# Second x loaded behind the constants and half split by GpSimd, with small products moved inside the mixing stage

## The chip, the cores and the metric

One core of a Trainium2 chip runs the kernel. A time is the device time of one launch in microseconds (us), and smaller is better. The core's engines each run a program of their own and meet at semaphores: TensorE (PE; its weight loads are listed as PEld), VectorE (DVE), ScalarE (ACT) and GpSimd (POOL). SyncE (SP) issues all DMAs of this kernel from one queue; 16 DMA engines carry them out.

## The reference, cut to what matters

Four conditioned layers are added in turn to x, which is 32 x 128 x 2048 (batch element, channel, position). Layers 0, 2 and 3 mix eight 128x128 weight matrices per batch element; layer 1 is a grouped convolution with 9 taps.

```python
def mixed(x, embedding, W0, b0, W1, b1, W2, b2, weight, bias_k):   # layers 0, 2, 3
    h = gelu(embedding @ W0 + b0); h = gelu(h @ W1 + b1)
    att = softmax(h @ W2 + b2, axis=-1)                 # 32 x 8
    agg_w = einsum('bk,koi->boi', att, weight[..., 0])  # 32 x 128 x 128
    return einsum('boi,bih->boh', agg_w, x) + (att @ bias_k)[:, :, None]

def conv(x, c, weight, c_weight, bias):                 # layer 1: 4 groups, 9 taps, padding 4
    ctx = einsum('nd,od->no', c, c_weight)
    return conv1d(x, weight, groups=4) + ctx[:, :, None] + bias[None, :, None]

x = x + mixed(x, cond_128, ...)   # layer 0
x = x + conv(x, cond_128, ...)    # layer 1
x = x + mixed(x, cond_128, ...)   # layer 2
x = x + mixed(x, cond_128, ...)   # layer 3
```

## The kernel before, in words

**Algebra.** The identity of each residual is folded into the weights. With a0, a2 and a3 the mixed matrices plus identity, layer 0 is `a0 x + c0`, the convolution has one added to its centre tap, and layers 2 and 3 collapse into one matrix `m`, the product of a3 and a2, for each batch element. What is left per element is: layer 0 (4 x 12 products), the convolution (4 x 36) and the product with m (4 x 12). Biases become vectors: `c0`, `d` (context plus bias of the convolution), `c2`, and `e`, the bias of the last two layers.

**Precision.** Every operand of the large products is kept as a high and a low part. "Splitting" x means a cast into the high part (`x_hi`) and a subtraction that leaves the low part (`x_lo`). A large product is then three: high by high, low by high, high by low. Each x is split in two halves, h = 0 and 1.

**The opening stage.** (1) A small network gives the attention shares (`hidden`, `logits`). (2) `attention` on PE spreads the shares over the partitions; DVE masks them into `spread`, one piece per layer. (3) `mixtures` makes a0, a2 and a3 in 24 tiles ("mixing"), four lanes of 32 rows side by side, four products per tile. ACT or DVE copies each tile out of PSUM, by the table `BY_SCALAR`; seven banks go round, so tile t waits for the copy of tile t-7. Between the products lie the small ones of c0, c2 and the spread third attention (`biases`), and of e (`bias_e`, 2 + 8 products). (4) `quad_product` multiplies a3 by a2, four elements at a time: quads 0 to 3, then layer 0 of x(0), then quads 4 to 7. (5) From then on four lanes, two steps apart, run through the 32 elements: layer 0 of element n+1, the convolution of n, the product with m of n-1 inside it.

**a0's way through DRAM.** The mixed a0 lies the wrong way round for the grouped rows, so SP saves it (`a0_pairs`; the first pair alone, the other 15 later) and reads it back four times (`a0_rep`); GpSimd splits it (`split_a0`). m goes the same way.

**The first x's.** x(0) comes in two halves at the head of the queue, and GpSimd splits both. x(1) is loaded by `load(1)`, which SP issues behind the read-back of a0's first pair; ACT casts its halves (between the first copies of m) and DVE subtracts. Behind those subtractions DVE's program has `x1_out(0)`: it writes the low part of the output of x(0)'s layer 0. `layer0_steps(1, p)` waits for piece p of it (`x1_lo_done`), since both use the same PSUM bank. From x(2) on DVE splits each x alone.

**What sets the order.** Nothing is scheduled at run time: each engine's program is written out in order, and `in_turn` takes one product from each lane in rotation. SP's queue is served in the order written, with its waits in it.

Of the kernel before, what the change touches and what calls it, by code (L numbers as in the profile page):

```python
# [9 lines left out]
ACT = mybir.ActivationFunctionType  # L10
# [5 lines left out]
K = 8  # L16
PH = 4
G = 4
# [5 lines left out]
NL = 3  # L24
# [5 lines left out]
LANES = 4  # L30
MIXES = NL * NOG

BY_SCALAR = [t % 2 == 0 or t == 9 for t in range(MIXES)]
DIAGONAL = OG * (LANES - 1) + HO
DMA = 16
PAIR = 2
# [30 lines left out]
def cond_resid_kernel(nc, x, net, consts, mix, bias, conv, c_weight, w3, out):  # L67
    with ExitStack() as ctx:  # L68
# [198 lines left out]
        def _(sp):  # L267
# [56 lines left out]
            load_half(0, 1)  # L324
            sp.dma_start(w3_sb, w3.rearrange("p (k m) -> p k m", k=K)).then_inc(e_loaded, DMA)
            sp.dma_start(conv_f[:], conv).then_inc(conv_loaded, DMA)
            sp.wait_ge(d_ready, 1)
            sp.dma_start(d_dram, d_sb[:]).then_inc(d_saved, DMA)

# [1 line left out]
            sp.wait_ge(*mix_taken(NOG - 1))  # L331
            save(a0_all, a0_dram, 0, 1, a0_saved[0])
            replicate_a0(0, range(PH))
            load(1)
            save(a0_all, a0_dram, 1, B // PAIR, a0_saved[1])
            load(2)
            sp.wait_ge(d_saved, DMA)
# [31 lines left out]
        def _(pe):  # L369
# [14 lines left out]

            def attention():


                pe.wait_ge(consts_loaded, DMA)
                pe.wait_ge(shares_ready, 1)
                pe.matmul(att_ps.rearrange("p n b -> p (n b)"), shares[:].rearrange("q c k o -> q (c k o)"),  # L390
                          eye_sb[0:NB, 0:NB], start=True, stop=True).then_inc(att_made, 1)
                bias_d()
                pe.matmul(att_t_ps.rearrange("k n b -> k (n b)"), shares[:, 0, :, 0], eye_sb[0:NB, 0:NB], start=True,
                          stop=True).then_inc(att_t_made, 1)
# [51 lines left out]
                          start=True, stop=True)  # L446
                pe.matmul(c2_ps, bias_sb[:, 1, :], att_t[:, 1, :], start=True, stop=True).then_inc(c_made, 1)

            def bias_e(options):
                if 0 in options:  # L450
                    pe.wait_ge(e_loaded, DMA)
                    pe.wait_ge(c2_att_ready, 1)
                    for n in range(1, NL):
                        pe.matmul(e_ps, bias_sb[:, n, :], att_t[:, n, :], start=(n == 1), stop=False)
                for k in options:
                    mm = pe.matmul(e_ps, w3_sb[:, k, :], c2_att[:, k, :], start=False, stop=(k == K - 1))  # L456
                return mm

            def layer0_steps(n, p):

# [95 lines left out]
            logits()  # L556
            fill(8)
            attention()
            mixing = [mixtures(c) for c in range(LANES)]

            in_turn(mixing, 3 * G)
            biases()
            in_turn(mixing, 2 * G)
            bias_e(range(0, 4))
            in_turn(mixing)
            bias_e(range(4, K)).then_inc(e_made, 1)
            for m in range(4):
                quad_product(m)
            in_turn([layer0_steps(0, p) for p in range(PH)])
# [5 lines left out]
        def _(act):  # L575
# [12 lines left out]
            act.wait_ge(logits_less_max, 1)  # L588
            nc.scalar.activation(lexp[:], lsub[:], ACT.Exp, accum_out=lsum[:]).then_inc(exp_done, 1)

            def split_second_x_hi(h):
                act.wait_ge(x_loaded[1], DMA)

                act.wait_ge(x_hi_done, HALVES + h)
                nc.scalar.activation(x_parts(1, h)[0], x_sb[1][:, PER * h:PER * (h + 1)],  # L595
                                     ACT.Identity).then_inc(x_hi_done, 1)

            def x1_out(n, phases=range(PH)):
                for p in phases:
# [27 lines left out]
            for t in range(MIXES):  # L627
                if BY_SCALAR[t]:
                    mix_evacuate(t)
            m_evacuate(0)  # L630
            split_second_x_hi(0)
            m_evacuate(1)
            split_second_x_hi(1)
            m_evacuate(2)
            m_evacuate(3)
            act.wait_ge(bias_out, 1)
# [18 lines left out]
        @block.gpsimd  # L655
        def _(pool):
            nc.gpsimd.memset(ones_k[:], 1.0).then_inc(ones_set, 1)
            for j in range(2):
                for buf in (x1_hi[j], x1_lo[j]):
                    nc.gpsimd.memset(buf[:, :, 0:T + 2:T + 1].bitcast(F32), 0.0).then_inc(zero_cols, 1)  # L660

            def add_identity(n):

                pool.wait_ge(mix_loaded[n], DMA)
                for diagonal in mix_diagonal[n]:
                    nc.gpsimd.tensor_tensor(diagonal, diagonal, diagonal_sb.unsqueeze(1).to_broadcast([P, G, DIAGONAL]),
                                            ALU.add).then_inc(mix_eyed[n], 1)

            def split_first_x(h):
                pool.wait_ge(x_first[h], DMA)  # L670
                src, (hi, lo) = x_sb[0][:, PER * h:PER * (h + 1)], x_parts(0, h)
                nc.gpsimd.tensor_copy(hi, src).then_inc(x_hi_done, 1)
                pool.wait_ge(x_hi_done, h + 1)
                nc.gpsimd.tensor_tensor(lo, src, hi.bitcast(F32), ALU.subtract).then_inc(x_lo_done, 1)

            def split_a0(n):
                pair = n // PAIR
                src = a0_rep[:, pair % 2, :, n % PAIR, :]
                pool.wait_ge(a0_rep_loaded[pair % 2], DMA * PH * (pair // 2 + 1))
                wait(pool, l0_done, PH * (n - 1))  # L680
                nc.gpsimd.tensor_copy(a0_hi[n % 2][:], src).then_inc(a0_split, 1)  # L681
                pool.wait_ge(a0_split, 2 * n + 1)
                nc.gpsimd.tensor_tensor(a0_lo[n % 2][:], src, a0_hi[n % 2][:].bitcast(F32),
                                        ALU.subtract).then_inc(a0_split, 1)

            def split_m(n):
                pair = n // PAIR
                src = m_rep[:, pair % 2, :, n % PAIR, :]
                pool.wait_ge(m_rep_loaded[pair % 2], DMA * PH * (pair // 2 + 1))
                wait(pool, y_done, PH * (n - 1))  # L690
                nc.gpsimd.tensor_copy(m_hi[n % 2][:], src).then_inc(m_split, 1)
                pool.wait_ge(m_split, 2 * n + 1)
                nc.gpsimd.tensor_tensor(m_lo[n % 2][:], src, m_hi[n % 2][:].bitcast(F32),
                                        ALU.subtract).then_inc(m_split, 1)


            pool.wait_ge(consts_loaded, DMA)
            pool.wait_ge(shares_ready, 1)
            for n in range(1, NL):
                add_identity(n)  # L700
            for h in range(HALVES):
                split_first_x(h)
            split_a0(0)
            split_a0(1)
            pool.wait_ge(conv_loaded, DMA)
            for q in range(PH):

                centre = conv_f[:, PH + q, rows(q)]
                nc.gpsimd.tensor_tensor(centre, centre, eye32_sb, ALU.add).then_inc(pool_chain, 1)
            pool.wait_ge(pool_chain, PH)  # L710
            nc.gpsimd.tensor_copy(conv_hi[:], conv_f[:]).then_inc(conv_split, 1)
            pool.wait_ge(conv_split, 1)
            nc.gpsimd.tensor_tensor(conv_lo[:], conv_f[:], conv_hi[:].bitcast(F32), ALU.subtract).then_inc(conv_split, 1)
            for n in range(B):
                if n + 2 < B:
                    split_a0(n + 2)
                split_m(n)

        @block.vector
        def _(dve):  # L720
# [88 lines left out]
            dve.wait_ge(e_made, 1)  # L809
            nc.vector.tensor_copy(e_all[:], e_ps).then_inc(e_out, 1)  # L810

            split_x_lo(1, 0)
            split_x_lo(1, 1)
            dve.wait_ge(bias_out, 1)
            x1_out(0)
# [81 lines left out]
```

## Time and profile before

| what | us |
|---|---|
| median of 3 runs | 488.22 |
| lowest, highest | 486.46, 493.41 |
| the profiled execution's own time | 492.4 |
| its span, first to last instruction | 490.5 |
| PE busy in that span | 478.9 |
| DVE, ACT, POOL busy | 322.7, 249.3, 153.4 |

The profile shows one execution. Its time is 4.2 us over the median and lies inside the range of the three runs. A matmul of this kernel that reads full fp32 has two records in the trace for each product; one that reads split operands has one.

### The profile page before, as it was taken

The page shows a single profiled execution, that of the slowest core. Times are in us where ns is not written, and L with a number is a line of the kernel's source. Part 1 is how long each engine was busy: PE and PEld are TensorE (multiplying, and loading weights), DVE is VectorE, ACT ScalarE, POOL GpSimd, SP SyncE. Part 2 cuts the span into 40 slices and gives each one's busy share as a digit, 9 for nine tenths or more (in the row PEclk, how much of TensorE's full clock was granted, in tenths as well). Part 3 has the DMA queues.
Part 4 walks back from the last instruction along what each step waited for, and adds up shares of the span by engine and source line. Part 5 has one row for each costly group of instructions (what it writes and reads, how often), then busy time and mean ns, then how long its engine had stood idle before and what let it go on. Part 6 is the DMA issues. An engine that isn't in the chain of part 4 may idle for free.

```text
span 490.5 us, 17899 instructions
## 1 busy us (share of the span) xinstructions
PE 478.9 (98%) x8003; PEld 433.1 (88%) x8003; DVE 322.7 (66%) x408; ACT 249.3 (51%) x415; POOL 153.4 (31%) x151
## 2 busy tenths in 40 slices
PE   8989899999999999999999999999999999999995
PEld 8979788888888888888888888888999999999994
DVE  2666766767687676767787676768777676767423
ACT  3562455544454555544554555444545554445344
POOL 3577042423332241433223241433233142430010
PEclk9998999999999999999999999999999999999998
DMA  8697957565646777464757666464667657551124
GB/s 292 208 331 226 265 182 216 169 205 131 216 153 210 216 210 217 136 212 130 219 176 215 216 200 214 134 208 124 216 204 216 215 164 214 127 204 53 67 88 172
DMA packets 38956, 92.88 MB, mean 189 GB/s; under 512 B 4568, under 2 KB 25440, under 8 KB 34912
## 3 DMA queue, kind: packets, MB, share of 16 engines
q1 hardware_dynamic: 38880, 91.73, 60.3%
q8 instruction: 64, 1.05, 0.9%
q14 instruction: 12, 0.10, 0.1%
HBM read 53.95 MB, written 37.77 MB: 187 GB/s over the span
## 4 chain that ended last, share of the span: by engine, by line
PE 97%; issue 1%; DVE 1%; DMA 1%; DVEq 0%
PE cv_ps L495 59%; PE aux_ps L476 17%; PE aux_ps L518 16%; PE cv_ps L434 2%; PE cv_ps L421 1%; PE aux_ps L421 1%; PE cv_ps L518 1%; DVE m_all L731 1%; DMA m_rep<-in_net_dram 1%; PE cv_ps L400 0%; PE aux_ps L375 0%; PE cv_ps L375 0%; PE aux_ps L456 0%; DVEq L68 0%; PE aux_ps L390 0%
## 5 line engine op out<-in xcount | busy, mean ns | idle before, releaser
L495 PE MATMUL cv_ps<-x_hi,conv_hi 32*128 32x512 f32 x1536 | 325.4, 389 | 2.2 <-issue 2.2
L495 PE MATMUL cv_ps<-x_hi,conv_lo 32*128 32x512 f32 x1536 | 325.6, 391 | 0.0
L495 PE MATMUL cv_ps<-x_lo,conv_hi 32*128 32x512 f32 x1536 | 325.3, 391 | 0.0
L495 PEld LDWEIGHTS cv_ps<-x_hi,conv_hi 32*128 32x128 f32 x1536 | 233.6, 183 | 12.4 <-issue 2.6
L495 PEld LDWEIGHTS cv_ps<-x_lo,conv_hi 32*128 32x128 f32 x1536 | 234.1, 184 | 11.5
L495 PEld LDWEIGHTS cv_ps<-x_hi,conv_lo 32*128 32x128 f32 x1536 | 233.8, 183 | 7.3
L764 DVE SCALAR_TENSOR_TENSOR x_lo<-cv_ps,d_all,x_hi 128x512 fp32r<-128x512 f32 x128 | 87.3, 745 | 138.7 <-ACT x_hi L609 138.7
L619 ACT ACTIVATE y_all<-aux_ps,e_all 128x512 f32<-128x512 f32 x124 | 75.1, 688 | 136.4 <-PE aux_ps L518 136.4
L476 PE MATMUL aux_ps<-x_hi,a_hi 32*128 32x512 f32 x512 | 118.1, 396 | 1.6 <-issue 1.6
L476 PE MATMUL aux_ps<-x_hi,a_lo 32*128 32x512 f32 x512 | 117.5, 392 | 0.0
L476 PE MATMUL aux_ps<-x_lo,a_hi 32*128 32x512 f32 x512 | 117.5, 392 | 0.0
L518 PE MATMUL aux_ps<-x_hi,m_hi 32*128 32x512 f32 x496 | 114.6, 388 | 0.0
L518 PE MATMUL aux_ps<-x_hi,m_lo 32*128 32x512 f32 x496 | 114.2, 388 | 0.0
L518 PE MATMUL aux_ps<-x_lo,m_hi 32*128 32x512 f32 x496 | 113.7, 385 | 0.0
L609 ACT ACTIVATE x_hi<-cv_ps,d_all 128x512 fp32r<-128x512 f32 x128 | 77.5, 689 | 67.7 <-PE cv_ps L495 67.7
L738 DVE TENSOR_TENSOR x_lo<-x_sb,x_hi 128x1024 fp32r<-128x1024 f32 x62 | 89.4, 1443 | 7.3 <-ACT x_hi L595 5.2
L755 DVE SCALAR_TENSOR_TENSOR x_lo<-aux_ps,c_all,x_hi 128x512 fp32r<-128x512 f32 x128 | 87.3, 746 | 1.6
L681 POOL CAST a_hi<-a_rep 128x512 fp32r<-128x512 f32 x32 | 27.0, 845 | 189.6 <-DMA a_rep<-a_pairs 121.0
L601 ACT ACTIVATE x_hi<-aux_ps,c_all 128x512 fp32r<-128x512 f32 x128 | 77.7, 690 | 15.7 <-PE aux_ps L476 15.7
L476 PEld LDWEIGHTS aux_ps<-x_hi,a_hi 32*128 32x128 f32 x512 | 80.2, 185 | 4.8 <-issue 1.8
L476 PEld LDWEIGHTS aux_ps<-x_hi,a_lo 32*128 32x128 f32 x512 | 80.5, 187 | 3.6
L518 PEld LDWEIGHTS aux_ps<-x_hi,m_lo 32*128 32x128 f32 x496 | 79.5, 183 | 2.9
(103 smaller groups left out, 540.5 us busy)
## 6 DMA issues: line engine op xcount, KB each, us to landing
x_sb<-in_x_dram SPq DMA_DIRECT2D x31, 1024.0 KB, 6.5
out_dram<-y_all SPq DMA_DIRECT2D x62, 512.0 KB, 7.6
a_rep<-a_pairs SPq DMA_DIRECT2D x64, 128.0 KB, 7.3
m_rep<-m_pairs SPq DMA_DIRECT2D x64, 128.0 KB, 6.1
a_pairs<-a_all SPq DMA_DIRECT2D x1, 1920.0 KB, 12.5
m_pairs<-m_all SPq DMA_DIRECT2D x1, 1792.0 KB, 13.3
m_all<-in_mix_dram SPq DMA_DIRECT2D x2, 512.0 KB, 5.6
x_sb<-in_x_dram SPq DMA_DIRECT2D x2, 512.0 KB, 7.2
```

Of the source, the lines that this page charges most:

```text
L421: mm = pe.matmul(mix_ps[t % MIX_RING][:, P * j:P * (j + 1)], mix_f[layer][rows(c), G * h + j, :], spread[rows(c), layer].rearrange("p b o ...
L434: mm = pe.matmul(prep_ps[m % RING][:, P * k:P * (k + 1)], a23_all[0][:, n, :], a23_all[1][:, n, :], start=True, stop=True)
L476: mm = pe.matmul(aux_ps[:, p, :], w[n % 2][rows(p), g, :], a[rows(p), g % PER, :], start=(i == 0), stop=(i == steps - 1))
L495: mm = pe.matmul(cv_ps[:, g, :], w[rows(g), j, :], a[n % 2][rows(g), q, s:s + T], start=(i == 0), stop=(i == steps - 1))
L518: mm = pe.matmul(out_bank(n, p), w[n % 2][rows(p), g, :], a[n % 2][rows(p), g, :], start=(i == 0), stop=(i == steps - 1))
L601: nc.scalar.activation(x1_hi[n % 2][:, p, 1:T + 1], aux_ps[:, p, :], ACT.Identity, bias=c0_all[:, n:n + 1]).then_inc(x1_hi_done, 1)
L609: nc.scalar.activation(x2_hi[n % 2][:, g, :], cv_ps[:, g, :], ACT.Identity, bias=d_all[:, g, n:n + 1]).then_inc(x2_hi_done, 1)
L619: nc.scalar.activation(y_all[:, k % YBUFS, p % PER, :], bank[:, p, :], ACT.Identity, bias=e_all[:, n:n + 1]).then_inc(y_out, 1)
L681: nc.gpsimd.tensor_copy(a0_hi[n % 2][:], src).then_inc(a0_split, 1)
L738: nc.vector.tensor_tensor(lo, x_sb[n % 2][:, PER * h:PER * (h + 1)], hi.bitcast(F32), ALU.subtract).then_inc(x_lo_done, 1)
L755: nc.vector.scalar_tensor_tensor(x1_lo[n % 2][:, p, 1:T + 1], aux_ps[:, p, :], c0_all[:, n:n + 1], x1_hi[n % 2][:, p, 1:T + 1].bitcast(F32 ...
L764: nc.vector.scalar_tensor_tensor(x2_lo[n % 2][:, g, :], cv_ps[:, g, :], d_all[:, g, n:n + 1], x2_hi[n % 2][:, g, :].bitcast(F32), ALU.add, ...
```

## The change

Five edits, all ahead of the steady stage:

1. SP issues `load(1)` right behind the constants of the convolution; it no longer stands between a0's read-back and the second save of a0.
2. GpSimd splits half 0 of x(1), high and low, ahead of `split_a0(0)`. ACT casts half 1 alone, ahead of all copies of m, and DVE subtracts half 1 alone.
3. The product for `d` and the turned shares (`att_t`) leave `attention` and follow behind two rounds of mixing (`options`). One idle product of 256 columns (`fill(1)`) takes their place.
4. The ten products for `e`, before in a block of six and a block of four, are issued one per round in the last ten rounds of mixing.
5. ACT copies tile 17 of the mixing, which DVE copied before.

```diff
-BY_SCALAR = [t % 2 == 0 or t == 9 for t in range(MIXES)]
+BY_SCALAR = [t % 2 == 0 or t in (9, 17) for t in range(MIXES)]
...
             sp.dma_start(conv_f[:], conv).then_inc(conv_loaded, DMA)
+            load(1)
             sp.wait_ge(d_ready, 1)
...
             replicate_a0(0, range(PH))
-            load(1)
             save(a0_all, a0_dram, 1, B // PAIR, a0_saved[1])
...
+            def bias_e():
+
+                pe.wait_ge(e_loaded, DMA)
+                pe.wait_ge(c2_att_ready, 1)
+                for n in range(1, NL):
+                    pe.matmul(e_ps, bias_sb[:, n, :], att_t[:, n, :], start=(n == 1), stop=False)
+                    yield
+                for k in range(K):
                     mm = pe.matmul(e_ps, w3_sb[:, k, :], c2_att[:, k, :], start=False, stop=(k == K - 1))
-                return mm
+                    if k == K - 1:
+                        mm.then_inc(e_made, 1)
+                    yield
...
             attention()
+            fill(1)
             mixing = [mixtures(c) for c in range(LANES)]
 
-            in_turn(mixing, 3 * G)
+            in_turn(mixing, 2)
+            options()
+            in_turn(mixing, 10)
             biases()
-            in_turn(mixing, 2 * G)
-            bias_e(range(0, 4))
-            in_turn(mixing)
-            bias_e(range(4, K)).then_inc(e_made, 1)
+            in_turn(mixing, 5)
+            in_turn([*mixing, bias_e()])
...
+            split_second_x_hi()
             m_evacuate(0)
-            split_second_x_hi(0)
             m_evacuate(1)
-            split_second_x_hi(1)
             m_evacuate(2)
...
             for h in range(HALVES):
-                split_first_x(h)
+                split_x(0, h)
+
+            split_x(1, 0)
             split_a0(0)
...
-            split_x_lo(1, 0)
             split_x_lo(1, 1)
             dve.wait_ge(bias_out, 1)
             x1_out(0)
```

DVE at the end of the opening stage, before and then changed; `x2_hi1` and `x2_lo1` are the buffers that hold the split x(1), and `x1_lo0` is what layer 0 of x(1) waits for.

```order
L731 COPY m_all<-cv_ps 128x32x16 [waits mix_made] x2
L810 COPY e_all<-aux_ps 128x32 [waits e_made]
L738 TENSOR_TENSOR x2_lo1<-x_sb1,x2_hi1 128x1024 [waits x_lo_done,x_hi_done] x2
L755 SCALAR_TENSOR_TENSOR x1_lo0<-aux_ps,c0_all,x1_hi0 128x512 [waits x1_hi_done,bias_out]
L755 SCALAR_TENSOR_TENSOR x1_lo0<-aux_ps,c0_all,x1_hi0 128x512 [waits x1_hi_done] x3
```

```order
L737 COPY m_all<-cv_ps 128x32x16 [waits mix_made] x2
L816 COPY e_all<-aux_ps 128x32 [waits e_made]
L744 TENSOR_TENSOR x2_lo1<-x_sb1,x2_hi1 128x1024 [waits x_lo_done,x_hi_done]
L761 SCALAR_TENSOR_TENSOR x1_lo0<-aux_ps,c0_all,x1_hi0 128x512 [waits x1_hi_done,bias_out]
L761 SCALAR_TENSOR_TENSOR x1_lo0<-aux_ps,c0_all,x1_hi0 128x512 [waits x1_hi_done] x3
```

One of two subtractions of 128x1024 is gone from DVE ahead of the four pieces; the copies of m in front of it are one fewer in all (tile 17).

POOL in the same stage, before and then changed: the split of x(0)'s last half, then a0's.

```order
L672 CAST x_hi1<-x_sb0 128x1024 [waits x_first1]
L674 TENSOR_TENSOR x_lo1<-x_sb0,x_hi1 128x1024 [waits x_hi_done]
L681 CAST a0_hi0<-a0_rep 128x512 [waits a0_rep_loaded0]
L683 TENSOR_TENSOR a0_lo0<-a0_rep,a0_hi0 128x512 [waits a0_split]
L681 CAST a0_hi1<-a0_rep 128x512 [waits a0_rep_loaded0]
```

```order
L676 CAST x_hi1<-x_sb0 128x1024 [waits x_first1]
L678 TENSOR_TENSOR x_lo1<-x_sb0,x_hi1 128x1024 [waits x_hi_done]
L676 CAST x2_hi1<-x_sb1 128x1024 [waits x_loaded1]
L678 TENSOR_TENSOR x2_lo1<-x_sb1,x2_hi1 128x1024 [waits x_hi_done]
L685 CAST a0_hi0<-a0_rep 128x512 [waits a0_rep_loaded0]
```

Two instructions have come in front of a0's split, and the first of them waits for the load of x(1).

PE at the end of the mixing stage (`L421`, now `L423`, are mixing products; `L456`, now `L459`, are the products for e), before and then changed.

```order
L454 MATMUL aux_ps<-att_t,bias_sb 128x32
L456 MATMUL aux_ps<-c2_att,m_rep 128x32 x4
L421 MATMUL aux_ps<-spread,a0_rep 128x128 [waits mix_out_v]
L421 MATMUL cv_ps<-spread,a0_rep 128x128
L421 MATMUL aux_ps<-spread,a0_rep 128x128 x3
L421 MATMUL cv_ps<-spread,a0_rep 128x128 [waits mix_out_a]
```

```order
L459 MATMUL aux_ps<-c2_att,m_rep 128x32
L423 MATMUL aux_ps<-spread,a0_rep 128x128 [waits mix_out_v]
L423 MATMUL cv_ps<-spread,a0_rep 128x128
L423 MATMUL aux_ps<-spread,a0_rep 128x128 x2
L459 MATMUL aux_ps<-c2_att,m_rep 128x32
L423 MATMUL aux_ps<-spread,a0_rep 128x128
```

The block of four is taken apart; between two products for e there now lie up to four mixing products.

## Rows read from the trace of the kernel before

**Rows 1.** Page, part 1: busy us, share of the span, instructions.
```profile
PE 478.9 (98%) x8003; PEld 433.1 (88%) x8003; DVE 322.7 (66%) x408; ACT 249.3 (51%) x415; POOL 153.4 (31%) x151
```

**Rows 2.** The chain that ended last, in order: start, us, what.
```profile
10.09 2.18 PE cv_ps L421 x24
...
20.61 2.50 DVE m_all L731 x4
23.25 3.81 PE cv_ps L434 x32
...
33.82 1.64 issue
35.46 4.76 PE aux_ps L476 x35
...
58.35 2.17 issue
```

**Rows 3.** Timeline of ACT, then DVE: start, us, instruction, idle before, releaser.
```profile
27.27 1.06 ACT L595 ACTIVATE x_hi<-x_sb 128x1024 fp32r<-128x1024 f32 x1 [2.27 <-DMA x_sb<-in_x_dram]
30.62 2.43 ACT L601 ACTIVATE x_hi<-aux_ps,c_all 128x512 fp32r<-128x512 f32 x4
28.37 6.32 DVE L738 TENSOR_TENSOR x_lo<-x_sb,x_hi 128x1024 fp32r<-128x1024 f32 x2 [5.17 <-ACT x_hi L595]
34.62 2.71 DVE L755 SCALAR_TENSOR_TENSOR x_lo<-aux_ps,c_all,x_hi 128x512 fp32r<-128x512 f32 x4
```

**Rows 4.** Windows: stretch, length, busy of each engine, PEclk, DMA share, GB/s.
```profile
36.00:37.00 1.00, 1.00 (x7) 0.89 (x8) 1.00 (x3) 0.00 (x0) 0.00 (x0) 0.59 0.43 150
37.00:39.00 2.00, 2.00 (x21) 2.00 (x22) 1.97 (x3) 0.00 (x0) 1.54 (x2) 0.50 0.04 15
39.00:40.00 1.00, 1.00 (x19) 1.00 (x15) 1.00 (x2) 0.00 (x0) 1.00 (x1) 0.70 0.76 227
10.00:14.00 4.00, 4.00 (x61) 3.98 (x64) 2.04 (x6) 1.36 (x3) 3.85 (x5) 1.00 1.03 424
14.00:15.00 1.00, 1.00 (x26) 1.00 (x24) 0.84 (x2) 0.71 (x2) 1.00 (x2) 1.00 0.77 286
```

**Rows 5.** Timeline of SP's queue: start and length of an issue.
```profile
6.45 0.50 SPq L326 DMA_DIRECT2D conv_f<-in_conv_dram  x1
15.95 0.33 SPq L279 DMA_DIRECT2D a_pairs<-a_all  x1
17.64 1.76 SPq L286 DMA_DIRECT2D a_rep<-a_pairs  x4
19.45 0.43 SPq L275 DMA_DIRECT2D x_sb<-in_x_dram  x1
```

**Rows 6.** DMA issues: KB each, median us from issue to landing.
```profile
conv_f<-in_conv_dram SPq DMA_DIRECT2D x1, 768.0 KB, 9.2
```

**Rows 7.** Timeline of PE and DVE in the mixing stage.
```profile
9.14 0.53 PE L404 MATMUL aux_ps<-m_rep,cw_sb 128*128 128x32 f32 x2
9.39 0.69 DVE L769 TENSOR_TENSOR spread<-aux_ps,consts_sb 128x128 f32<-128x128 f32 x3 [0.90 <-PE aux_ps L390]
21.85 1.08 PE L456 MATMUL aux_ps<-c_att,m_rep 128*128 128x32 f32 x8
```

**Rows 8.** Timeline of POOL.
```profile
15.92 2.36 POOL L674 TENSOR_TENSOR x_lo<-x_sb,x_hi 128x1024 fp32r<-128x1024 f32 x1
23.04 0.61 POOL L681 CAST a_hi<-a_rep 128x512 fp32r<-128x512 f32 x1 [4.76 <-DMA a_rep<-a_pairs]
23.73 1.27 POOL L683 TENSOR_TENSOR a_lo<-a_rep,a_hi 128x512 fp32r<-128x512 f32 x1
```

**Rows 9.** One line's instructions: DVE's subtractions, durations ns min/median/max.
```profile
L738 DVE TENSOR_TENSOR x_lo<-x_sb,x_hi x62: 1224/1226/4284, 28.4 to 450.0; 128x1024 fp32r<-128x1024 f32 x62
```

**Rows 10.** Mixing products (line 421): durations ns min/median/max; one answer until 12 us, one from 16.1 us.
```profile
L421 PE MATMUL cv_ps<-spread,m_all x26: 416/416/577, 10.0 to 11.9; 32*128 32x128 f32 x26
...
L421 PE MATMUL cv_ps<-spread,m_all x22: 270/270/372, 16.2 to 18.4; 32*128 32x128 f32 x22
```

## What was predicted before the change was run

> **What bounds the kernel now.** I read the page first, then the chain of waits, then the timeline of each engine around the places where the chain leaves PE. PE is busy 98% of the span [rows 1]: the steady stage is bound by PE alone, and the change doesn't touch it. What an edit of the opening can give lies in the pieces of the chain that are not PE at full speed. The chain has three of them [rows 2]: 2.50 us of DVE's copies of the last mixing tiles, 1.64 us of standstill at 33.82, and 2.17 us at 58.35.
>
> The piece at 33.82 is the one that the change aims at. The chain calls it "issue", so its cause must be read from the order of the instructions. Layer 0 of x(1) may not begin before the first low piece of x(0)'s output. DVE begins these four pieces at 34.62 and needs 2.71 us for them, 0.68 each [rows 3], so the first is there at 35.30; PE goes on at 35.46 [rows 2]. Their input was there long before: ACT's first high piece began at 30.62. DVE was busy from 28.37 to 34.69 with the two subtractions of x(1) [rows 3], and these began late since x(1) landed late: ACT's cast sat idle for the DMA until 27.27 [rows 3]. One of the two took 4.28 us where the median is 1.23 [rows 9].
>
> The standstill has a tail. The four lanes start one by one as DVE delivers, and the granted clock then falls: 0.59 of full in the microsecond from 36, 0.50 for two more, 0.70 in the next [rows 4]. 0.50 is the lower level, 1.2 GHz instead of 2.4. In full-speed work that is 0.41 + 1.00 + 0.30 = 1.7 us lost.
>
> **The change part by part.**
>
> *x(1) loaded early.* The queue is full until about 14.8: a DMA share of 1.03 at 424 GB/s until 14, then 0.77 of one microsecond [rows 4], and the convolution's constants land at 6.45 + 9.2 = 15.65 [rows 5, 6]. x(1) is 1 MB; at 424 GB/s it adds 2.5 us, so the engines are free at 17.3 and x(1) is there at about 18.1 instead of 27.27. It was issued at 19.45 before; the second save of a0 gets that slot, and everything behind it comes up to 2.5 us sooner. The first that waits for it is layer 0 of x(2), a whole convolution later: zero.
>
> *POOL's two new instructions.* The subtraction takes 2.36 us, as on x(0); the cast I estimate at twice the 0.61 of a 128x512 one, 1.2 [rows 8]. From 18.1 the pair ends at 21.7. POOL stands idle 4.76 us before a0's split at 23.04 [rows 8], so this costs nothing as long as x(1) lands before about 19.6. a0's split of the first element ends at 23.73 + 1.27 = 25.00, and PE wants it at 23.25 + 3.81 = 27.06 [rows 2, 8]: 2 us of slack.
>
> *a0's first save.* It was issued at 15.95 and its read-back at 17.64 [rows 5], on an empty queue. Now x(1) stands before it until 17.3. I take the landing of the save as 0.9 us later (0 if it overtakes, 1.7 if it starts only then and takes its 1.7 again), so the split ends at 25.9, still inside the slack.
>
> The Trainium skill speaks against this edit: "DMA: Bandwidth & Descriptors", Queues, rings and completion order, says that on each DMA engine descriptors are consumed in ring order, so the save cannot pass x(1). By that rule the gentle end, 0, is excluded; the value above doesn't rest on it.
>
> *DVE's list.* With half 0 gone to POOL and half 1 cast by ACT right behind its last tile, DVE's one subtraction begins near 23.6 and ends between 24.8 (1.23) and 27.9 (4.28) [rows 9], in either case before 30.62. The four low pieces follow ACT's high ones from 31.2 on. With the same 0.68 each the first is there at 31.9 and the fourth at 34.0, where PE wants them from about 34.3 (33.82 and the 0.5 of the two paragraphs below). **The standstill of 1.64 us and the 1.7 us of the clock go.**
>
> Beside that subtraction POOL now splits a0, where before it split the convolution's constants. The row at 4.28 was such a case [rows 9]. The Trainium skill has a rule: "GPSIMD Engine Reference", Key points, says that GpSimd shares its SBUF interfaces with VectorE and contends with instructions of two SBUF inputs. If a0's split stretched by as much as the 4.28 row, from 1.27 to some 3 us, it would end at 27.6 instead of 25.9; the stretch itself I bound by the rows (none to 3.05 us in all) and take 0.7.
>
> *d and the turned shares.* Before, they fill PE from 9.14 until mixing begins at 10.09 [rows 2, 7]. The first `spread` is ready at 9.39 + 0.28 (the group of three takes 0.69), and mixing can begin near 9.75. The two products are then done behind it, at the same price of 0.9. So the work is the same, PE stands or idles on `fill` in 9.14 to 9.75, and what follows comes up to 0.6 us later. Between 0 and +0.6, I take +0.2, since from 16 us on the copies set the pace there (seven banks, two engines) and they absorb some.
>
> *e's products one by one, tile 17.* A block of four takes 1.08 [rows 7], 0.27 each, singly the same work. Before, the block in the middle starves the copies, and DVE then has four in a row (2.50, 0.62 each) that PE's quads wait for until 23.25 [rows 2], while the last block runs from 21.85 to 22.93 [rows 7]. Now the last mixing product comes about one e-product before the end of the same PE work, 22.93 - 0.27 = 22.66; one copy of 0.62 ends at 23.3. That is no gain. Each e-product also cuts the four lanes apart: between 0 and 0.27 each for the eight, so 0 to 2.2. I take 0.3, near the lower end, since inside the block the eight records come at 1.08 / 8 = 0.135 us each, so even there little is lost to filling and draining. Tile 17 on ACT: nothing, ACT has room. Together +0.3.
>
> **Sum**, against the profiled execution's own 492.4: -1.64 - 1.7 + 0.2 + 0.3 = -2.8, so 489.6. That execution lies 4.2 over the median of 488.22. I can't see a median execution, so I subtract the same from the median, a little less because in some executions the clock may not have fallen: 488.2 - 2.6 = **485.6**.
>
> **The rivals.**
>
> 1. *The wait goes, but the clock's part was only in this execution.* The clock fell once the lanes had crept for 3 us; a run that starts otherwise may not fall. Then only 1.64 - 0.5 = 1.1 is saved: 487.1. For it speaks that the profiled run was a slow one; against it that the creeping is set by DVE and comes in all.
> 2. *a0 late (slower).* x(1) takes a0's place in the queue, POOL starts on it late, and DVE's subtraction stretches a0's split. It decides where layer 0 of x(0) would start, 27.06 + 0.5: if a0's read-back lands past 25.4 instead of 23.04, the first split (1.88) and its stretch (0.7) end at 28.0, PE stands again and, if it stands as long as it did at 33.82, the clock falls again. At a landing of 27.5 the loss is 2.5 + 1.7 = 4.2 against a gain of 3.3 - 0.5: 488.2 + 1.4 = 489.6. For it: the round trip is the one thing the early load can hurt. Against: 4.4 us later than now would have to come from 1 MB that needs 2.5.
> 3. *Mixing stays slow longer.* A mixing product takes 416 ns until 12 us and 270 ns from 16.2 [rows 10], though the granted clock is listed as 1.00 throughout. If gaps of single e-products and at 9.5 put off that change, each microsecond of delay costs half a microsecond; 4 us and the full 2.2 for the cuts cancel the gain: 488.2 - 3.3 + 0.2 + 2.2 + 2 = 489.3. The Trainium skill, "TensorE: Matmul & The Clock Gate", What's actually happening, says the default state is throttled and activity releases it; by that rule less activity there costs, more (an earlier start) gains, about 1 us either way.
> 4. *The standstill at 58.35.* PE waits 2.17 us [rows 2] with no semaphore in its order at that place. Instructions come by DMA too. In another arrangement of the traffic it may be gone: 485.6 - 2.2 = 483.4; or fall elsewhere, with no change.
> 5. *The change doesn't do what it says*: x(1) lands late all the same. Then DVE still has one subtraction less, about 1.2 to 3 us: 486.5.
>
> **Chances.** Forecast 0.50 (own range 484.3 to 487), rival 1: 0.17, rival 2: 0.10, rival 3: 0.08, rival 4: 0.12, rival 5: 0.03. The executions of before spread over 7 us by themselves, and the median of three carries 1 or 2 of that. So the range goes from rival 4's end less one, 482.5, to rivals 2 and 3, 489.8. The 2% that a measurement of this kernel can tell from no change are 9.8 us, more than any case here moves: within 2% 0.97, faster 0.02, slower 0.01.
>
> **What would show it.** Right: no "issue" piece near 34, DVE's four low pieces starting within 1 us of ACT's first high piece, a granted clock of 1.00 from 33 to 41, x(1)'s cast by POOL at 18 to 19, a0's first cast near 24. Wrong: a0's cast past 25, PE idle before layer 0 of x(0), quads later than 24.5, or mixing products still at 416 ns past 16 us. The prediction fails if a gain here is given back later, which I think unlikely, since behind 58.35 the chain has no further piece off PE worth a row [rows 2].

## The result, and the profile after

| | median us | range | executions |
|---|---|---|---|
| before | 488.96 | 486.46 to 494.75 | 22 |
| after | 493.94 | 491.77 to 496.62 | 22 |

After over before is 1.0109 [1.0089, 1.0128]: 1.1% slower, by 5.0 us in the medians, where 485.6 was forecast. The profiled execution after took 496.62, its span 494.8. Ratios here leave out executions more than 1.5% above the fastest of their kernel, while medians contain all; part of before's executions lie that high, so for kernels close to it the two can differ by half a per cent.

Page, part 1 and the clock line of part 2, to be held against [rows 1]:

```profile
PE 486.2 (98%) x8004; PEld 460.1 (93%) x8004; DVE 318.7 (64%) x406; ACT 252.1 (51%) x415; POOL 151.7 (31%) x153
PEclk9969999999999999999999999999999999999998
```

PE is no less full than before, yet busy 7.3 us longer. The busy share says nothing here. The third digit of the clock (a slice of 12.4 us from 24.7 on) says that PE was full at a lower rate. The chain, against [rows 2]:

```profile
30.07 5.93 PE cv_ps L436 x32
35.99 3.00 PE aux_ps L481 x43
38.99 3.77 PE cv_ps L436 x32
42.76 3.11 PE aux_ps L481 x42
```

The standstill near 34 is gone, as forecast: layer 0 of x(1) (42.76) follows the second quads at once. The quads start at 30.07 instead of 23.25, though, and take 5.93 instead of 3.81. The windows before them, with the columns of [rows 4]:

```profile
20.00:24.00 4.00, 4.00 (x67) 3.47 (x62) 1.79 (x3) 2.97 (x5) 3.25 (x2) 1.00 0.64 199
24.00:28.00 4.00, 4.00 (x33) 3.06 (x26) 1.38 (x2) 0.69 (x3) 2.43 (x3) 0.53 1.08 380
28.00:32.00 4.00, 3.69 (x15) 3.29 (x16) 1.95 (x3) 1.47 (x2) 3.90 (x6) 0.50 1.01 356
32.00:36.00 4.00, 4.00 (x29) 3.88 (x28) 0.00 (x0) 1.79 (x3) 3.92 (x2) 0.69 0.55 168
```

The granted clock falls from 1.00 to 0.50 (1.2 GHz instead of 2.4) while PE is listed busy 4.00 of 4.00 us. This is not the fall of [rows 4], which came behind a wait. PE's timeline shows what it does there: single products for e (`L459`, both records) with mixing products between them.

```profile
21.76 0.41 PE L459 MATMUL aux_ps<-c_att,m_rep 128*128 128x32 f32 x2
22.10 0.37 PE L423 MATMUL aux_ps<-spread,a_rep 32*128 32x128 f32 x1
...
22.53 0.41 PE L459 MATMUL aux_ps<-c_att,m_rep 128*128 128x32 f32 x2
...
27.83 0.64 PE L459 MATMUL aux_ps<-c_att,m_rep 128*128 128x32 f32 x2
...
29.12 0.64 PE L459 MATMUL aux_ps<-c_att,m_rep 128*128 128x32 f32 x2
```

A round with one product for e in it takes 0.77 us at the full clock and 1.29 at the lower one. So two costs are to be told apart: the cuts, by which I mean the breaks in the four lanes' rounds that a product of full height makes, and the clock. Behind them stand the other four edits.

### The profile page after: what moved, and what is told of

It is laid out like the page before. It is cut to its first block, busy times and chain, and to the rows that moved or that the text cites. A ratio compares the mean times of both kernels' runs of the same rounds, so it can differ in the third digit from the quotient of the medians.

```text
span 494.8 us, 17899 instructions
## 1 busy us (share of the span) xinstructions
PE 486.2 (98%) x8004; PEld 460.1 (93%) x8004; DVE 318.7 (64%) x406; ACT 252.1 (51%) x415; POOL 151.7 (31%) x153
## 3 DMA queue, kind: packets, MB, share of 16 engines
q8 instruction: 64, 1.05, 0.9%
## 4 chain that ended last, share of the span: by engine, by line
PE 98%; DMA 1%; DVE 0%; issue 0%; DVEq 0%
PE cv_ps L500 55%; PE aux_ps L481 18%; PE aux_ps L523 16%; PE cv_ps L436 2%; PE cv_ps L423 2%; PE aux_ps L423 1%; PE aux_ps L459 1%; PE cv_ps L523 1%; DMA m_rep<-in_net_dram 1%; PE cv_ps L402 0%; PE aux_ps L375 0%; PE cv_ps L375 0%; PE aux_ps L447 0%; DVEq L68 0%; DVE m_all L737 0%
## 5 line engine op out<-in xcount | busy, mean ns | idle before, releaser
L500 PE MATMUL cv_ps<-x_hi,conv_lo 32*128 32x512 f32 x1536 | 321.1, 391 | 0.7 <-issue 0.7
L500 PE MATMUL cv_ps<-x_lo,conv_hi 32*128 32x512 f32 x1536 | 320.5, 391 | 0.0
L500 PE MATMUL cv_ps<-x_hi,conv_hi 32*128 32x512 f32 x1536 | 320.5, 390 | 0.0
L481 PE MATMUL aux_ps<-x_hi,a_hi 32*128 32x512 f32 x512 | 113.6, 391 | 0.0
L481 PE MATMUL aux_ps<-x_hi,a_lo 32*128 32x512 f32 x512 | 113.3, 388 | 0.0
L481 PE MATMUL aux_ps<-x_lo,a_hi 32*128 32x512 f32 x512 | 113.3, 388 | 0.0
L744 DVE TENSOR_TENSOR x_lo<-x_sb,x_hi 128x1024 fp32r<-128x1024 f32 x61 | 84.7, 1389 | 2.1
L481 PEld LDWEIGHTS aux_ps<-x_hi,a_lo 32*128 32x128 f32 x512 | 75.9, 184 | 1.8
L481 PEld LDWEIGHTS aux_ps<-x_hi,a_hi 32*128 32x128 f32 x512 | 75.8, 183 | 1.9
L481 PEld LDWEIGHTS aux_ps<-x_lo,a_hi 32*128 32x128 f32 x512 | 75.8, 183 | 1.9
```

What stands on the lines that cost most here:

```text
L481: mm = pe.matmul(aux_ps[:, p, :], w[n % 2][rows(p), g, :], a[rows(p), g % PER, :], start=(i == 0), stop=(i == steps - 1))
L500: mm = pe.matmul(cv_ps[:, g, :], w[rows(g), j, :], a[n % 2][rows(g), q, s:s + T], start=(i == 0), stop=(i == steps - 1))
L744: nc.vector.tensor_tensor(lo, x_sb[n % 2][:, PER * h:PER * (h + 1)], hi.bitcast(F32), ALU.subtract).then_inc(x_lo_done, 1)
```

## The experiments

Diffs are against "after" or "before" as named; all kernels compute the whole reference. "Before" ran beside each. I call its executions over 490 us the long ones; the two of them that were profiled have a wait near 34 us.

**e's products in blocks again, all else as after.**

```diff
-            in_turn(mixing, 5)
-            in_turn([*mixing, bias_e()])
+            in_turn(mixing, 8)
+            for_e = bias_e()
+            in_turn([for_e], 6)
+            in_turn(mixing)
+            in_turn([for_e])
```

> The changed kernel with e's ten products in two blocks again (6 and 4, as before), all else as changed. Theory S (the single products for e are the loss: each cuts the four lanes apart, the granted clock falls to 0.5 in that stretch and stays there through the first quads): the stretch from the first product for e to the first quad goes back from 9.4 us to about 5, quads 0 to 3 from 5.9 to 3.8 us, so 6 us less than the changed kernel: about 488. Rival O (moving d and the turned shares behind two rounds puts off the rise of the clock, from about 16 us to 21 us, and that is the loss): mixing products still last 416 ns until 20 us, and the time stays within 1 us of the changed kernel's 494.

Measured 488.61 (486.56 to 491.95), 5.3 under after; ratio to before 1.000 [0.9971, 1.0029]. In its chain and windows:

```profile
23.59 3.81 PE cv_ps L436 x32
...
20.00:24.00 4.00, 3.80 (x62) 3.56 (x61) 2.06 (x4) 2.96 (x6) 3.22 (x2) 1.00 0.40 117
24.00:28.00 4.00, 4.00 (x41) 3.88 (x43) 1.22 (x1) 2.44 (x5) 2.65 (x4) 1.00 1.07 376
```

The clock stays at 1.00 and the quads take 3.81. This one edit holds the whole loss of the change; what the others cost and bring adds up to about nothing.

**`d` and the turned shares ahead of mixing again; then that and the blocks together.** In the first the diff against after is

```diff
-            fill(1)
+            options()
...
-            in_turn(mixing, 2)
-            options()
-            in_turn(mixing, 10)
+            in_turn(mixing, 12)
```

and the second has the diff above as well: the early x(1), its split by GpSimd and tile 17 are all that it keeps.

> The changed kernel with the product for d and the turned shares ahead of mixing again and without the extra idle product; e's products stay single. Theory O: the clock rises near 16 us again, mixing ends 2 to 5 us sooner, and the time goes to 488 to 490. Theory S: the clock still falls at the single products, the first quad starts at 26 us or later, and the time stays above 492.

> The changed kernel with both edits of the order on TensorE undone; the early load of x(1), its split by GpSimd, and tile 17 on ScalarE stay. If the saving that was predicted for the early x(1) is real, the wait before layer 0 of x(1) (1.64 us) and the fall of the clock behind it (1.7 us) are gone and the time is 485.5 to 486.5, below the kernel before by 3. If an early x(1) costs a0's round trip through DRAM more than it brings, the first layer 0 waits for a0's split and the time is 489 or more.

Measured 492.17 (490.76 to 493.97), 1.0076 [1.0051, 1.0102], for the first; 486.75 (485.95 to 490.07), 0.998 [0.9958, 1.0002], for the second. Single products cost 5.4 in this pair, and moving `d` and the shares costs 1.8 (after less the first) or 1.9 (the blocks less the second). The second kernel's chain has neither wait nor slow stretch:

```profile
20.72 1.90 DVE m_all L738 x3
22.62 0.14 issue
22.75 3.81 PE cv_ps L436 x32
26.56 3.38 PE aux_ps L481 x48
29.94 3.77 PE cv_ps L436 x32
33.71 3.10 PE aux_ps L481 x42
```

**Each of the two edits alone, on before.** `bias_e` and the rounds as in the change, nothing else of it; then `fill(1)` and `options()` as in the change, nothing else.

> The kernel before with e's products single as the only edit. Theory S: 3 to 6 us slower than before, 492 to 495, with a granted clock under 0.8 between 20 and 30 us. Theory O: the clock has risen by 16 us as before, the single products cost at most their own switching, and the time is within 1 us of before's 489.

> The kernel before with the product for d and the turned shares behind two rounds of mixing and one idle product in their place, nothing else. Forecast price: +0.2 us. From the profiles of e_blocks and both_back, where the first copy starts 1.14 us later (13.27 against 12.13 in before): +1 to +2 us.

The first: 492.43 (489.17 to 495.17), 1.0098 [1.0066, 1.013], 4.0 over before beside it (488.47). The second: 489.26 (487.22 to 494.92), 1.0031 [1.0002, 1.0061], 1.3 over (487.98). So the loss needs no early x(1): the granted clock falls on the kernel before too, in the windows below. The price is under 5.4, and a reason for it stands in the trace: the kernel before's own wait near 34 is gone, since PE comes to layer 0 of x(1) only at 37.87. The windows of the first:

```profile
24.00:28.00 4.00, 3.69 (x17) 3.59 (x18) 0.45 (x2) 1.42 (x2) 3.85 (x8) 0.50 1.07 381
28.00:32.00 4.00, 4.00 (x34) 3.77 (x36) 3.74 (x2) 2.86 (x5) 3.92 (x2) 0.71 1.01 378
```

For the second, the place is ACT's first copy, in before and then in the second kernel:

```profile
12.13 0.60 ACT L583 ACTIVATE a_all<-cv_ps 128x512 f32<-128x512 f32 x1 [4.14 <-PE cv_ps L421]
```

```profile
13.17 0.60 ACT L588 ACTIVATE a_all<-cv_ps 128x512 f32<-128x512 f32 x1 [5.20 <-PE cv_ps L423]
```

The products moved behind two rounds end there in the same price, but what the copies wait for comes 1.04 us later. The same stands in after (13.27); with the products back ahead it is 12.17 (e single) and 12.10 (blocks).

**How many cuts does it take?** e two products at a time, in five cuts, `d` and the shares ahead of mixing:

```diff
+            in_turn(mixing, 8)
+            for_e = bias_e()
+            in_turn([for_e], 2)
+            for _ in range(4):
+                in_turn(mixing, 2)
+                in_turn([for_e], 2)
+            in_turn(mixing)
```

> As att_first, with e's products two at a time between two rounds of mixing: five cuts instead of ten. In the profiles a round with a single product takes 0.77 us at the full clock, against about 0.25 for a round and 0.25 for a product in a block, so a cut costs 0.27. Theory C: five cuts fewer save 1.3 us, and if the clock then holds, 3 us more: 488 to 491. If only the position in the program matters and not the number of cuts: 492, as att_first.

Measured 487.99 (486.40 to 490.38), 1.0001 [0.9966, 1.0037]: 4.2 less than ten singles, 1.2 more than blocks of six and four (before itself read 487.90 beside this run and 488.47 beside those two). In its profile the clock falls in one window alone, and rises again under the quads; that execution took 490.35, at the upper end of the twelve, so a median one may lose less:

```profile
24.00:28.00 4.00, 4.00 (x24) 4.00 (x23) 1.04 (x1) 1.19 (x2) 2.24 (x3) 0.57 1.03 353
28.00:32.00 4.00, 4.00 (x59) 3.23 (x57) 0.00 (x0) 1.20 (x2) 3.78 (x8) 1.00 1.07 373
```

**Can idle work hold the clock?** e singly, and behind each of its products one 128x256 idle product into a free bank:

```diff
-            in_turn([*mixing, bias_e()])
+            def idle_beside():
+                for i in range(K + NL - 1):
...
+                    pe.matmul(mix_ps[bank % MIX_RING][:, 0:2 * P], idle_sb[:, 0:P], idle_sb[:], start=True, stop=True)
+                    yield
+            in_turn([*mixing, bias_e(), idle_beside()])
```

> As att_first (e's products single, d and turned shares ahead of mixing), with one idle product of 128x256 zeros behind each product for e: more work on TensorE, at the same number of cuts. Theory C (half of the loss is the clock, which falls because the array does so little between the cuts): the granted clock stays 1.00 from 20 to 32 us, the quads take 3.8 us instead of 6.1, and the time falls by 1.5 to 3 us from att_first's 492.2 although ten products are added. Rival P (the clock falls whatever is put there, or the loss is all the switching): the same fall of the clock and 1 to 2 us more than att_first.

Measured 494.95 (492.86 to 497.05), 1.013 [1.0077, 1.0183], 2.8 over the same kernel without them. The fall comes later (0.91 in the first window, 0.65 without the idle products) and is as deep, so the added work is paid and buys nothing:

```profile
20.00:24.00 4.00, 4.00 (x42) 3.00 (x42) 0.69 (x1) 1.79 (x3) 2.73 (x2) 0.91 0.41 108
24.00:28.00 4.00, 4.00 (x18) 3.02 (x15) 1.17 (x2) 1.54 (x2) 2.63 (x4) 0.50 1.06 369
28.00:32.00 4.00, 4.00 (x19) 3.80 (x19) 2.16 (x3) 0.60 (x1) 3.94 (x6) 0.50 1.07 383
```

**No cut at all.** All ten products behind the last mixing product, with the early x(1) (run twice), and on before alone:

```diff
-            in_turn(mixing, 5)
-            in_turn([*mixing, bias_e()])
+            in_turn(mixing)
+            in_turn([bias_e()])
```

> As both_back, with all ten products for e in one block behind the last mixing product: no cut inside mixing, and the copies of the last tiles run beside the block. Theory C: the first quad starts 0 to 0.7 us sooner than in both_back (22.75), clock 1.00, time 486 to 487. If the block of products without mixing beside it lets the clock fall (it has 32 columns each): the quads at half rate, 488 to 490.

> e_last once more (early x(1), split by GpSimd, tile 17 on ScalarE, e's products in one block at the end): 486 to 487, with a narrower spread than before, since no execution has the wait at 34 us.

> The kernel before with all ten products for e in one block behind the last mixing product, nothing else changed. If the order of e's products is worth something by itself (no starving of the copies between two blocks), 0.3 to 0.8 us under before. Its difference from e_last_b is the worth of the early x(1): 3.3 by the forecast, 1 to 1.7 if the wait at 34 us is there in some executions only.

With the early x(1): 486.52 (485.69 to 487.50), 0.997 [0.994, 0.9999], and again 486.41 (485.91 to 487.36), 0.9966 [0.9938, 0.9993]. This is the lowest median of the study: 0.3% under before, with intervals that end just below 1, and 1.5% under after. The block stands where PE would wait for the last copies anyway: the quads follow it without a wait. Its chain, from the first run, and then the block in PE's timeline:

```profile
20.48 1.90 PE aux_ps L459 x16
22.38 3.65 PE cv_ps L436 x32
```

```profile
20.41 1.97 PE L459 MATMUL aux_ps<-c_att,m_rep 128*128 128x32 f32 x16
```

On before alone: 490.93, in two groups, four executions at 485.03 to 485.40 and eight at 490.37 to 495.25; 0.9996 [0.9949, 1.0042]. Its profile fell in the upper group and has the wait at 32.48 for 2.56 us. Held against the two runs above, it gives the worth of the early load with GpSimd's split and tile 17: without them about 485.3 or 490 and more, with them 485.7 to 487.5 in all 23 executions.

**Tile 17 back on DVE, in the fastest kernel.** One entry of `BY_SCALAR` less.

> e_last with tile 17 of the mixing copied by VectorE again. If the edit was free, as priced: within 0.3 us of e_last_b. If ScalarE relieves the last copies: 0.3 to 0.7 us slower.

486.91 (486.14 to 487.74), 0.9977 [0.9958, 0.9997]: 0.4 to 0.5 more than with it on ACT, little more than the two runs of one kernel can tell.

**x(1) late, still split by GpSimd.** `load(1)` back behind a0's read-back, in the kernel with both other edits undone.

> As both_back, with the load of x(1) back at its old place behind a0's read-back; GpSimd still splits half 0, so it now waits for x(1) ahead of a0's split. If the place of the load is what saves the time: x(1) lands at 27, GpSimd's a0 split comes only behind it at 31 or later, TensorE stands before the first layer 0, and the time is 490 to 494. If the early load does nothing: 486.8.

Measured 495.37 (493.74 to 498.17), 1.0144 [1.009, 1.0198], 8.6 over its counterpart. POOL's cast of x(1) waits for the load, a0's split waits behind it, and PE stands:

```profile
26.31 1.04 POOL L677 CAST x_hi<-x_sb 128x1024 fp32r<-128x1024 f32 x1 [7.58 <-DMA x_sb<-in_x_dram]
27.43 2.34 POOL L679 TENSOR_TENSOR x_lo<-x_sb,x_hi 128x1024 fp32r<-128x1024 f32 x1
29.72 0.60 POOL L686 CAST a_hi<-a_rep 128x512 fp32r<-128x512 f32 x1
```

```profile
26.96 5.66 issue
```

Half of x(1) on POOL is only good together with the early load.

**The given kernels once more, unchanged,** to see how far one profile speaks for all executions: before twice, after once.

> The kernel before, unchanged, once more under the profiler. The first profile lay 4.2 us over the median. If the fall of the clock behind the wait at 34 us and the standstill of 2.17 us at 58 us belong to that execution and not to the kernel, one or both are missing here and the span is 485 to 488; if they belong to the kernel, both are here and the early x(1) should have brought 3.3 us, not the 1.7 that both_back measured.

> The same as before_a, a second look. The wait before layer 0 of x(1) (1.6 us) should be here in each, since it comes from the order of the loads.

> The changed kernel, unchanged, once more under the profiler. If the single products for e set the fall of the clock, it falls here too between 20 and 26 us. The first rise, at 21 us in the first profile and near 16 us in all kernels run since, is expected near 16 us here; if it is at 21 us again, moving d and the turned shares puts it off.

Before took 493.25 and 486.24. The wait near 34 is in the first, 2.62 us long, and not in the second. What differs is when x(1) lands, told by ACT's first cast of it; in order, the first and the second:

```profile
28.51 1.06 ACT L595 ACTIVATE x_hi<-x_sb 128x1024 fp32r<-128x1024 f32 x1 [3.73 <-DMA x_sb<-in_x_dram]
```

```profile
26.60 1.06 ACT L595 ACTIVATE x_hi<-x_sb 128x1024 fp32r<-128x1024 f32 x1 [1.88 <-DMA x_sb<-in_x_dram]
```

The landing alone would not reach PE. Without a stretch, by my estimate from the rows, DVE's second subtraction in the first of the two would end at 29.95 + 1.05 + 1.23 = 32.2, ACT's first high piece is there at 31.86 + 0.61 = 32.5, and a low piece takes 0.68: 33.2, before PE stops at 33.59. What holds DVE is POOL's subtraction of the convolution's constants. DVE, then POOL, in the first:

```profile
29.60 5.84 DVE L738 TENSOR_TENSOR x_lo<-x_sb,x_hi 128x1024 fp32r<-128x1024 f32 x2 [6.63 <-ACT x_hi L595]
30.06 4.30 POOL L713 TENSOR_TENSOR conv_lo<-conv_f,conv_hi 128x1536 fp32r<-128x1536 f32 x1
```

and in the second, where DVE's second subtraction has begun before POOL's:

```profile
29.12 2.20 DVE L738 TENSOR_TENSOR x_lo<-x_sb,x_hi 128x1024 fp32r<-128x1024 f32 x1 [0.20 <-ACT x_hi L595]
30.33 4.34 POOL L713 TENSOR_TENSOR conv_lo<-conv_f,conv_hi 128x1536 fp32r<-128x1536 f32 x1
```

In the five traces in which POOL's began first (the two long ones of before, `d` and the shares moved on before, e last on before, e single on before), DVE's second subtraction ended 1.08 or 1.09 us behind POOL's, at 34.28 to 35.44; here it ended at 31.32. So the landing decides which engine comes first, and that decides over a wait. This is read from six traces; no run moved POOL's subtraction alone. Of the 7.0 us between the two executions 2.6 are the wait, 3.4 the clock (0.96, 0.50 and 0.68 in the windows of 4 us from 32 to 44) and 0.55 a standstill at 60.26.

After took 493.7, with its quads at 27.73 for 6.14 us and the same fall:

```profile
20.00:24.00 4.00, 4.00 (x46) 3.21 (x46) 0.69 (x1) 2.08 (x4) 3.05 (x2) 0.80 0.48 141
24.00:28.00 4.00, 3.69 (x19) 2.81 (x14) 1.80 (x4) 1.54 (x2) 3.12 (x4) 0.50 1.08 386
28.00:32.00 4.00, 4.00 (x20) 4.00 (x20) 1.67 (x1) 1.08 (x2) 3.86 (x7) 0.50 1.00 357
32.00:36.00 4.00, 4.00 (x53) 3.56 (x55) 0.00 (x0) 1.31 (x3) 3.44 (x1) 0.92 0.86 221
```

## Why the prediction was wrong

**The sum by edits**, in medians: early x(1) with its split and tile 17 gave 486.75 - 488.47 = -1.7 (before's median over the 35 executions that ran beside them), the options cost +1.9, e's single products +5.4. That makes +5.6; measured were +5.0 against before's 488.96, and +5.5 against these 488.47. The forecast had -3.3, +0.2 and +0.3 in the same places, with tile 17 at nothing.

**The step that failed is e's products one by one**: "between 0 and 0.27 each for the eight, so 0 to 2.2. I take 0.3, near the lower end". It failed twice.

- *Its size.* A round of mixing without a product for e takes about 0.25 us (seven rounds between 20.15 and 21.85 before), a product for e 0.25 (eight in 1.97 behind the mixing). Together 0.50, where the single round takes 0.77: 0.27 a cut, the upper bound, and 2.2 for eight. In the chains less of it arrives. From the first mixing product that reads `a_rep` to the first quad pass 9.79 us with `d` and the shares ahead and e single, 5.57 with the blocks; 2.8 of the difference are the clock, so 1.5 are the cuts. The second profile of after against its kernel in blocks gives 1.5 too, e single on before 1.7. The reason for the low end was the rate of the records inside a block of like products; that says nothing of a change from full-height products to four lanes of 32 rows and back.
- *Its kind.* No term had the clock fall under a busy PE. In the second profile of after the windows lose 0.20, 0.50, 0.50 and 0.08 of 4 us each: 0.8 + 2.0 + 2.0 + 0.3 = 5.1 us of full-speed work.

For the kernel with `d` and the shares ahead these two are read against its counterpart in blocks: 1.5 for the cuts and 1.4 + 2.0 + 1.7 = 5.1 for the clock (0.65, 0.50 and 0.57 in the windows from 20 to 32), less the 0.4 by which its layer 0 of x(0) is shorter (2.99 against 3.38). That is 6.2; the two profiled executions lie 6.3 apart (492.25 and 485.95), the medians 5.4. So about a quarter of the loss is the cuts and the rest the clock.

That the single products bring the fall is shown, on both kernels; that fewer cuts bring a shorter one, too. What in the alternation the chip answers to is not: PE was listed busy all along, and idle products between did not help. The listed busy time may hide that fewer rows of the array work; that stays open.

**x(1) early.** The effect came as forecast: no wait near 34, clock 1.00 from 36 on, DVE's low pieces (39.87) 0.8 behind ACT's high ones (39.07); POOL's cast of x(1) came at 19.84, a little behind the 18 to 19 of the forecast. The cause was seen in part. The prediction laid DVE's lateness to the landing and took the row of 4.28 us as a bound; that row, DVE held by POOL's subtraction, is what made PE wait, and the early x(1) takes DVE out of POOL's way. The size was off, because the wait of [rows 2] isn't there in every execution, and the fall of the clock not behind every wait. "The creeping is set by DVE and comes in all" was wrong: in the kernel before with `d` and the shares moved, PE waits 1.66 us at 34.10 and creeps in the same way, but the clock stays, and the execution took 489.1:

```profile
36.00:40.00 4.00, 4.00 (x55) 3.41 (x58) 3.96 (x6) 0.80 (x3) 1.57 (x1) 1.00 0.37 112
```

That is rival 1's mechanism, in some executions. In the median the edit gives 1.7; against a long execution it gives 4 and more, against a short one it costs about 1 (486.4 against 485.3 with e last), and nothing here shows why.

**a0's save** lies inside its bounds: 3.1 us from issue to landing instead of 1.7, 1.4 later where 0.9 was taken. Its own issue came 1.1 later too, so a0's first cast stands at 25.44, past the 25 that the prediction had named as a sign of being wrong. SP's issues of the save and of the read-back, and then POOL:

```profile
17.09 0.33 SPq L279 DMA_DIRECT2D a_pairs<-a_all  x1
20.22 1.76 SPq L286 DMA_DIRECT2D a_rep<-a_pairs  x4
```

```profile
19.84 1.04 POOL L676 CAST x_hi<-x_sb 128x1024 fp32r<-128x1024 f32 x1 [1.38 <-DMA x_sb<-in_x_dram]
25.44 0.61 POOL L685 CAST a_hi<-a_rep 128x512 fp32r<-128x512 f32 x1 [2.12 <-DMA a_rep<-a_pairs]
```

The Trainium skill's rule of ring order ("DMA: Bandwidth & Descriptors", Queues, rings and completion order) agrees with this: the save of 128 KB did not land before x(1), whose landing released POOL at 19.84. a0's split held up nobody, since the quads came 6.8 us late. It was near to deciding, though: in one run with e in one block, layer 0 of x(0) waits 0.34 us for it (26.37 where the quads end at 26.03). Rival 2's mechanism is real in another kernel than the one forecast: with x(1) late and GpSimd splitting it, PE stood 5.66 us and the clock fell as it said.

**The shared port.** DVE's one subtraction took 1.25 us, so nothing stretched there (2.07 in the second profile); POOL's cast of the convolution's constants beside it did, 2.34 us where the kernel with both edits undone has 1.47:

```profile
30.16 2.34 POOL L717 CAST conv_hi<-conv_f 128x1536 fp32r<-128x1536 f32 x1
```

```profile
29.22 1.47 POOL L718 CAST conv_hi<-conv_f 128x1536 fp32r<-128x1536 f32 x1
```

That GpSimd and VectorE contend when VectorE's instruction has two SBUF inputs is what the Trainium skill states ("GPSIMD Engine Reference", Key points). The trace agrees, with the stretch now on the one engine and now on the other; no one waited for this one, where in the kernel before PE did.

**`d` and the turned shares.** "Between 0 and +0.6, I take +0.2" was below what three pairs showed, 1.3 to 1.9. Two full-height products stand there among the mixing, and the first copies come 1.0 to 1.1 later. The copies did not absorb this; they passed it on.

**Rival 3** was nearest to what happened, and named the second mechanism too: mixing products at 416 ns for longer. After and then its second profile:

```profile
L423 PE MATMUL cv_ps<-spread,m_all x20: 416/416/577, 17.7 to 20.4; 32*128 32x128 f32 x20
```

```profile
L423 PE MATMUL cv_ps<-spread,m_all x12: 270/270/372, 16.6 to 17.5; 32*128 32x128 f32 x12
```

In one the change comes past 20 us, in the other at about 16, as before. The quads start 2.3 us apart (30.07 and 27.73), half a microsecond for each, as the rival priced it. But the second execution lost nothing there and was still slow (493.7), so the late change explains a part of the 496.62 alone. The rival's 489.3 lacked the later fall of the clock. The Trainium skill ("TensorE: Matmul & The Clock Gate", What's actually happening) has a default of throttled and activity that releases it. Taken by the listed busy time, that rule would have let PE keep its clock; the trace has 0.50 at 4.00 of 4.00 busy, and the measurement decides.

**Rival 4.** The standstill at 58.35 (2.17 us) is in no profile of after. Of the two further ones of before one has 0.55 at 60.26, the other none; e last on before has 2.15 at 59.05, and the kernel with e in pairs, which loads x(1) early, 1.33 at 56.97. So it is no gain of the change; it comes and goes, and its cause stays open.

## What to carry to other kernels

A small product of another shape is not free because PE would do it anyway: put it where PE waits already, in one block, and count a price per cut, from a row where the shapes alternate, not from inside a block. When one row of a group takes three times its median, look at what ran beside it before you lay the delay to its late start. Take two or three profiles of the kernel before where its executions spread by over 1%, and ask which of its waits are in all of them; an edit that removes a wait of some executions narrows the spread and moves the median by a part of it. An engine given new work ahead of old work takes over the new work's wait.

## What the runs showed of the hardware that was not expected

- The granted clock fell from 1.00 to 0.50 with PE listed busy all the time, in four kernels with single products for e, between 21 and 25 us, and came back under the quads. In the kernel with pairs it fell at 24, behind 0.32 us of idle time that the kernel before has there too. With blocks of six and four it did not fall there.
- Ten idle products of 128x256 between did not hold it (0.91, 0.50, 0.50 in the windows from 20 to 32).
- Going from four lanes of 32 rows to one full-height product and back costs 0.27 us at the full clock by the length of a round; over the whole stretch eight such cuts cost 1.5 to 1.7.
- A VectorE subtraction of 128x1024 that began behind GpSimd's of 128x1536 took 4.2 to 4.3 us instead of 1.23 and ended 1.08 or 1.09 behind it, in five traces.
- The same wait (1.64 and 1.66 us at 34) was followed by a fall of the clock to 0.50 in one execution and by 1.00 in another.
- The same 1 MB load, issued at the same place, reached ACT at 26.60, 27.27 or 28.51 in three executions of one kernel.
